# Down projections of combinations 4 to 7 in seven half products, with chunk 10 finished ahead of the loop and chunk 11 in its first pair

## What is computed

```python
Wg = dequant_nvfp4(gate_W_packed, gate_scales)   # [4096, 512]
Wu = dequant_nvfp4(up_W_packed, up_scales)       # [4096, 512]
Wd = dequant_nvfp4(down_W_packed, down_scales)   # [512, 4096]
gate = jnp.einsum('th,nh->tn', xt, Wg)
up = jnp.einsum('th,nh->tn', xt, Wu)
gelu = jnp.tanh(0.7978845608028654 * (gate + 0.044715 * gate ** 3)) * gate * 0.5 + gate * 0.5
inter = gelu * up
out = jnp.einsum('tn,hn->th', inter, Wd)
```

## Time and profile before

| | |
|---|---|
| median of 3 runs | 1121.4 us (1120.69 to 1121.43) |
| profiled execution, its own time | 1121.95 us |
| its span, first to last instruction | 1119.8 us |
| TensorE busy | 1109.5 us, 99% of the span |
| VectorE, GpSimd, ScalarE busy | 851.6, 651.0, 492.9 us |
| granted TensorE clock, mean | 1.000 |
| chain that ended last | 93% TensorE |

### The profile page before, as it was taken

How to read it: one execution, slowest core, us unless ns; L and a number is a source line. 1 busy time by engine, 2 the same in 40 slices (tenths; PEclk the granted TensorE clock), 3 DMA queues, 4 the chain that set the end, 5 groups by cost and what they waited for, 6 DMA issues and landing times.

```text
span 1119.8 us, 22346 instructions
## 1 busy us (share of the span) xinstructions
PE 1109.5 (99%) x8842; PEld 864.5 (77%) x8842; DVE 851.6 (76%) x1491; ACT 492.9 (44%) x1148; POOL 651.0 (58%) x665
## 2 busy tenths in 40 slices
PE   8999999999999999999999999999999999999999
PEld 5666656556457677788888888888888888888886
DVE  7788666457777766688988898889888888886664
ACT  4442344254244344444544455445444544454332
POOL 2376545137684765656775577567756775676330
PEclk9999999999999999999999999999999999999999
DMA  9021111000112222223322232323232323231222
GB/s 307 5 69 47 38 34 42 11 10 1 38 57 76 76 103 103 83 107 115 123 96 105 104 114 95 109 100 114 95 127 88 116 102 126 94 115 76 76 76 76
DMA packets 30232, 96.65 MB, mean 86 GB/s; under 512 B 3440, under 2 KB 3760, under 8 KB 23472
## 3 DMA queue, kind: packets, MB, share of 16 engines
q1 hardware_dynamic: 30128, 95.23, 24.1%
HBM read 63.73 MB, written 31.49 MB: 85 GB/s over the span
## 4 chain that ended last, share of the span: by engine, by line
PE 93%; POOL 2%; DVE 2%; issue 2%; ACT 1%; DMA 0%; SPq 0%; DVEq 0%; POOLq 0%; ACTq 0%
PE ps L627 44%; PE ps L696 19%; PE ps L457 9%; PE ps L588 7%; PE ps L736 7%; PE ps L423 1%; PE ps L549 1%; PE ps L532 1%; PE ps L556 1%; PE ps L543 1%; PE ps L467 1%; PE ps L523 1%; DMA WR<-wqkv 0%; POOL WR L1669 0%; DVE wf L1358 0%
## 5 line engine op out<-in xcount | busy, mean ns | idle before, releaser
L627 PE MATMUL ps<-XT,WR 128*128 128x256 f16 x1344 | 183.3, 273 | 0.0
L627 PE MATMUL ps<-REG,WR 128*128 128x256 f16 x1344 | 183.3, 273 | 0.0
L1020 ACT COPY load<-ps 128x256 f32<-128x256 f32 x168 | 62.4, 371 | 225.6 <-PE ps L627 225.2
L627 PEld LDWEIGHTS ps<-REG,WR 128*128 128x128 f16 x1344 | 130.0, 98 | 21.0
L627 PEld LDWEIGHTS ps<-XT,WR 128*128 128x128 f16 x1344 | 131.5, 98 | 15.4
L1303 DVE SCALAR_TENSOR_TENSOR X<-ps,X 128x512 f32<-128x512 f32 x161 | 108.2, 684 | 16.1 <-PE ps L696 13.8
L1020 ACT COPY bigB<-ps 128x256 f32<-128x256 f32 x168 | 62.5, 372 | 129.4 <-PE ps L627 129.4
L1591 POOL TENSOR_TENSOR ihl_s<-fw,ihl_s 128x512 f16<-128x512 f32 (+1 forms) x46 | 49.5, 1088 | 116.7 <-ACT ihl_s L923 116.7
L1375 DVE TENSOR_TENSOR bigB<-bigB,ps 128x256 f32<-128x256 f32 x168 | 69.7, 415 | 59.8 <-ACT bigB L1020 37.0
L1375 DVE TENSOR_TENSOR load<-load,ps 128x256 f32<-128x256 f32 x168 | 68.8, 414 | 45.3 <-ACT load L1020 31.8
L627 PE MATMUL ps<-REG,bigA 128*128 128x256 f16 x672 | 91.7, 273 | 1.0 <-ACT bigB L1020 1.0
(11 more groups left out here) (231 smaller groups left out, 2515.5 us busy)
## 6 DMA issues: line engine op xcount, KB each, us to landing
kept<-X SPq DMA_DIRECT2D x26, 1024.0 KB, 4.5
X<-kept SPq DMA_DIRECT2D x26, 1024.0 KB, 5.7
load<-codes SPq DMA_DIRECT2D x48, 256.0 KB, 2.7
load<-scales SPq DMA_DIRECT2D x48, 256.0 KB
bigA<-cla SPq DMA_DIRECT2D x14, 256.0 KB, 3.1
X<-x SPq DMA_DIRECT2D x3, 1024.0 KB, 13.0
WR<-wqkv SPq DMA_DIRECT2D x2, 1024.0 KB, 9.8
y<-X SPq DMA_DIRECT2D x2, 1024.0 KB, 4.8
```

Of the source, the lines that this page charges most:

```text
L627: mm = eng.matmul(half_bank(kind, name), w(wp, kt), x(xp, kt), start=(first and n == 0), stop=(n == 5), skip_group_check=True)
L1020: eng.copy(start, half_bank(kind, name)).then_inc(s_snap, 1)
```

## The change

Combinations 4 to 7 join those whose down work is done in seven half products. For this chunks 10 and 11 get the form of the other down chunks: chunk 10 is of the first kind and is finished ahead of the loop (codes between tiles 13 and 14, scalings behind tile 15 on VectorE; cast on ScalarE and low half on GpSimd as the last thing ahead of the loop), and chunk 11 gets the sums and is finished in pair 8, its sums in pair 9. The counts of pairs of chunks, the two float buffers that chunks use in turn, the loads and the release of bank 7 follow.

```diff
-SEVEN = tuple(range(8, 31))
+SEVEN = tuple(range(4, 31))
...
 def plain(k):
 
-    return k < 6 or k in (10, 11, LAST)
+    return k < 6 or k == LAST
...
 def pair_count(k):
 
-    return k % 6 // 2 + 1 + (3 * (k // 6) - 4 if k >= 12 else 0)
+    return 3 * (k // 6 - 1) + k % 6 // 2 + 1
 
 def finished_in(k):
 
-    return k - 2 if k < 12 else 8 * (k // 6) + (-6, -5, -3, -2, -1, 0)[k % 6]
-
-FINISHED = {finished_in(k): k for k in range(10, 48)}
+    return 8 * (k // 6) + (-6, -5, -3, -2, -1, 0)[k % 6]
+
+FINISHED = {finished_in(k): k for k in range(11, 48)}
 
 def second_before(m):
 
     g = m // 8
-    if m % 8 == 1 and m > 9:
+    if m % 8 == 1:
         return 6 * g + 5
...
-            return wfs[pair_count(k) % 2 if k >= 12 else 0]
+            return wfs[1 - pair_count(k) % 2 if k >= 12 else 0]
...
-            return tb[:, :] if k < 6 else PS[7 if k < 10 else 5][:, :].bitcast(I32)
+            return tb[:, :] if k < 6 else PS[7 if k < 11 else 5][:, :].bitcast(I32)
...
-            banks.freed[7] = [(s_dq, 60)]
+            banks.freed[7] = [(s_dq, 66)]
...
@@ ScalarE, dq_mul and dq_first
-                    if g == 1:
-                        ac.wait_ge(s_mm["v"], 16)
-                        ac.wait_ge(s_tlo, 4)
...
+                elif k == 10:
+                    ac.wait_ge(s_tlo, 4)
...
@@ ScalarE, ahead of the loop and in it
             inter_high(15)
+            dequant(10)
             for m in range(8, NI // 2):
...
-                if m < 12 or m % 8 == 7 and m in FINISHED:
+                if m in FINISHED and (m < 12 or m % 8 == 7):
                     dequant(FINISHED[m])
...
@@ VectorE, dq_finish
-                elif k in (12, 14):
+                elif k >= 12:
                     dv.wait_ge(s_kept[1], 16)
-                    dv.wait_ge(s_wlo, WLO[11][1])
-                    dv.wait_ge(s_wsum, 2)
-                elif k > 14:
                     dv.wait_ge(s_wsum, pair_count(k) - 2)
...
@@ VectorE, ahead of the loop and in it
             token_sums(1)
-            for i in range(13, 16):
-                act_tile(i)
+            act_tile(13)
+            dq_bits(10)
+            act_tile(14)
+            act_tile(15)
+            dq_finish(10)
             for m in range(8, NI // 2):
...
                 combine("gate", m, "C12")
                 if m < 12:
-                    dq_bits(FINISHED[m])
+                    if m in FINISHED:
+                        dq_bits(FINISHED[m])
...
                 combine("up", m, "C11")
-                if m < 12:
+                if m < 12 and m in FINISHED:
                     dq_finish(FINISHED[m])
...
@@ GpSimd, ahead of the loop and in it
             token_low(1)
+            dequant(10)
             for m in range(8, NI // 2):
...
-                elif k and k > 11:
+                elif k:
                     if c == 0:
                         dq_difference(k)
                     dq_first_sums(k)
                     dequant(k)
...
@@ SP's queue
             eng.dma_start(kept[2], X1[:, 8:12, :]).then_inc(s_kept[0], 16)
+            load_chunk(11)
...
                 if m < 12:
-                    load_codes(m + 3)
-                    load_scales(m + 3)
+                    if m in FINISHED:
+                        load_chunk(FINISHED[m] + 1)
```

More of the change, by code:

```diff
@@ L987, in dq_sums @@
                     ac.wait_ge(s_kept[(g + 1) % 2], 16)
-                    ac.wait_ge(s_tlo, 16)
+                    if g % 2 == 0:
+                        ac.wait_ge(s_tlo, 16)
                 if k == LAST + 1:
```

## The result

The changed kernel takes 1126.5 us (median of 5 runs, 1124.86 to 1127.81), the kernel before 1121.4 (5 runs, 1120.69 to 1121.85). The ratio is 1.0045 [1.0031, 1.0060]: **slower by 5 us**. I had forecast 1123.1 in a range up to 1125.8, so the result lies above the range. The profiled execution took 1126.26 us, span 1124.5, which is 4.7 more than the span before.

A forecast was written before the change was run, and what follows sets the result against it. TensorE's work plus its few gaps was taken as the bound. +4.2 (gap in pair 8) + 1.1 (pairs 10 to 12) - 3.6 (pairs 13 to 17) = +1.7 us, forecast 1123.1 from 1121.4; range 1120.0 to 1125.8.

The forecast's parts named there:

- The matmuls: Half products in place of plain down products in pairs 13 to 17: 68.12 us for 71.75, minus 3.6.
- Chunk 10 ahead of the loop: Pair 8's first snapshot waits behind chunk 10's scalings and cast, so P6 waits from 328.0 to 332.15: plus 4.2 us.
- rival 1: Loop's start: scalings before tile 15 let ScalarE reach the first snapshot in time; sum -3.9, 1117.5 us; chance 0.10.
- rival 3: Behind pair 8's new gap the clock falls and TensorE works slowly: 1.8 us on top, 1124.9 us; chance 0.12.
- +1.1: Pairs 10 to 12: 48.1 us against 47.06, as waits on GpSimd and VectorE outweigh the matmuls saved.
- 4.5 to 6.5 us of waiting: Pairs 11 and 12: TensorE's waiting while GpSimd, working without rest, makes four low halves per pair; 4.8 taken.
- Rival 2: VectorE and GpSimd stretch each other's token and operand sums: 2.4 us more in pairs 10 to 13, 1125.5; chance 0.23.
- P6 some 4 us behind P2: Sign in pair 8: P6 released late by ScalarE's snapshot, with VectorE's scalings of chunk 10 ending near 331.
- Pair 9 at 14.35: Sign that pair 9 keeps its length of 14.35 us, the extra work of chunk 11 being hidden.
- Pair 10 near 15.3: Sign of VectorE's load in pair 10, its last needed sum about 0.9 us late for TensorE.
- Pairs 11 and 12 together near 33: Sign of GpSimd busy from chunk 12's low half to the low halves of pair 11; length in us.
- A stretch behind the gap at half rate: Sign listed as proving the forecast wrong: TensorE at half rate behind pair 8's gap.

The follow-up runs named there:

- cast_late: Changed kernel with ScalarE's cast of chunk 10 moved behind pair 8's three gate snapshots, not ahead of the first; 1123.44 us, ratio 1.0018 to the kernel before.
- gpsimd_early: Changed kernel with GpSimd's token sums of block 3 moved ahead of chunk 12's low half in pair 10; 1125.74 us, ratio 1.0038 to the kernel before.
- chunks_only: Changed kernel with combinations 4 to 7 back in plain down products, chunks 10 and 11 still finished early (output differs); 1127.16 us.
- wait_40: Kernel before with 40 small ScalarE copies ahead of pair 8's first snapshot, to make a gap; 1127.45 us, ratio 1.0050.
- fill_gap: Changed kernel with 30 unused matmuls between P2 and P6 of pair 8, where TensorE waits for the snapshot; 1124.74 us.
- three_split: Changed kernel with chunk 10's cast late, GpSimd's block 3 sums early, VectorE's token sums in pairs 9 and 12 in two halves; 1120.43 us.
- late_spread: Changed kernel with chunk 10's cast behind pair 8's gate snapshots and VectorE's token sums four at a time in pairs 9 and 12; 1127.00 us.
- all_three: Changed kernel with chunk 10's cast late, GpSimd's block 3 sums early, and VectorE's token sums four at a time in pairs 9 and 12; 1123.92 us.

## Why the prediction was wrong

I forecast 1123.1; measured 1126.5. Step by step, against the profiled execution, whose sum I had put at +1.7 and which came out at +4.7.

**The matmuls.** -3.6 for pairs 13 to 17: measured 71.75 - 68.12 = 3.63. Right.

**Chunk 10 ahead of the loop.** +4.2 with P6 at 332.15; P6 came at 331.58 with the pair's start 0.47 earlier, so the gap is 4.04. The order of the chain, scalings, cast, snapshot, P6, was as worked out. Right, and rival 1 (cover at the loop's start) with it excluded. What I had not seen is that a part of the gap's price doesn't come back with its removal: without the gap (cast_late) pairs 9 to 12 grow by 2.1 us. That doesn't move the forecast, but whoever reads a gap's length as what its removal gives is wrong by 2 us here.

**The clock.** This is the first step that failed: rival 3, to which I gave 0.12, is what happened. I had worked out its price from the transposes as 1.8; the profile shows 1.68. That the price came so near is partly luck: three other profiles with such a gap lost 2.7 to 2.9. Nor is its source shown to be the clock: narrow windows of the trace of before, which I had not asked for, give a granted clock of 1.00 from 2 to 6 us too, where the slow transposes stand. The chance was wrong. I had kept it low because no row of the loop had such a gap, which is evidence for neither side. The Trainium skill's sentence (TensorE: Matmul & The Clock Gate, "Why this matters for your kernels") said what was to come: an idle gap of some microseconds between bursts of matmuls brings the lower level back. The runs agree with it: each of the four profiles with a gap of 3.4 to 3.6 us in pair 8 (after, gpsimd_early, chunks_only, wait_40) has 0.50 behind it, and fill_gap, with matmuls in the same place, 1.00.

**GpSimd and VectorE in pairs 10 to 12.** The second step that failed is the term "+1.1": measured +2.99. Pair 10 was put at 0.9 above 14.41 and has 1.2, with the wait where I had it. For pairs 11 and 12 I had "4.5 to 6.5 us of waiting ... I take 4.8", and 0.5 beside; they take 34.45, which is 6.9 above 27.51. The low half of pair 11's tile was to be ready 24.2 us after the pair's start if GpSimd was slowed as in the rows of before; TensorE's product that needs it starts at 400.08, 24.3 after 375.76. The end that I named as the upper one was met, though in part by luck: GpSimd began its stretch 0.56 us ahead of the pair and not 0.63 behind its start, and then took 1.3 us longer, since the four sums of token_sums(3) took 5.75 us in place of 4.48. I had moved off that end "since VectorE is less in GpSimd's way", a reason without a row. It was not so: VectorE is busy 16.98 of 17.36 us of that pair. Rival 2 (the two in each other's way, +2.4) comes close in size, and a part of its mechanism is there: the three operand sums from 378.40 take 3.98 us, 1.2 more than the 2.8 that I had counted. How much of TensorE's waiting comes from that, and how much from the sheer work, no run separates. Of the places of the waits I had some: 386.75 waits for GpSimd through the gelu, as 379.23 did before, and 400.08 for the low half. The start of pair 12 waits 1.06 us for token_low(2), which I didn't name, and in pair 11 two waits (0.68 and 1.03) are for VectorE's sums, for which I had put nothing.

**The sum.** +4.04 + 1.68 + 0.15 + 2.99 - 3.63 = +5.2, less 0.5 by which pair 8 began earlier: +4.7. Of the 3 us by which the profile misses the forecast's 1.7, the clock is 1.7 and pairs 10 to 12 are 1.9; 0.5 goes the other way. I had treated rivals 2 and 3 as ways that exclude each other, with 1125.5 and 1124.9; both came true at once, and the range had no case for their sum, 1123.1 + 2.4 + 1.8 = 1127.3.

**Signs that I had named.** "P6 some 4 us behind P2": 3.38 us of waiting, right. "Pair 9 at 14.35": 14.50. "Pair 10 near 15.3": 15.60. "Pairs 11 and 12 together near 33": 34.45. "A stretch behind the gap at half rate" was listed as what would prove me wrong, and did.

What stays open: how long and where the clock falls in the other runs of the changed kernel. They differ by 3 us, wider than those of the kernel before. The profiled run has a mean clock of 0.997, and its two stretches at half clock are 6.9 us together. By the same measure, an estimate, the run with 0.995 (1127.81 us) had some 11 us at half clock and the one with 0.998 (1124.86 us) some 4 or 5, but only one execution has a trace.

## What to carry to other kernels

Before work is put ahead of a loop on an engine that takes its instructions in order, follow the first instruction behind it to TensorE: here one cast, 0.5 us long but 2.7 us in waiting for VectorE, opened a gap of 4 us, and the gap opened a stretch at half clock that cost 1.7 to 2.9 more. Matmuls taken out are worth only what the engines that feed TensorE can follow: of 4.8 us, 0.6 arrived, since GpSimd and VectorE are the bound in three of the eight pairs, in two of them already before the change. Mishaps that don't exclude each other add up, so the range needs the case in which two of them come together.

## What the runs showed of the hardware

*The price of a fall differs for like gaps.* Behind 3.38 us without work the clock was at 0.50 until 335.5 in one profile (1.68 us lost), and until 336.2 to 337.2 in two others with 3.4 us (2.7 and 2.80 us lost) and in the one with 3.58 (2.89). In these three the granted clock was already below 1 in the gap itself (0.68 at 330 in wait_40), in the first only behind it.

*For shorter waits the traces go either way.* No fall behind waits of 0.60 and 1.72, nor behind 2.22 (fill_gap), 2.52 (three_split) and one of 2.40 (late_spread); a fall behind another of 2.40 and behind 3.16 (both all_three), and behind another of 2.22, which follows one of 1.82 seven us earlier (late_spread). Two waits of about 1 us, 1.9 apart, were followed by a fall in the changed kernel and not in fill_gap.

*Four token sums in a row on VectorE, each with two SBUF inputs, took 5.8 and 6.3 us beside a working GpSimd*, some 1.5 each, and two took 3.14 and 3.25; in the kernel before two took 1.41 three times and 3.19 once. The Trainium skill (SBUF — State Buffer, "SBUF: two separate sides") has such an instruction and one of GpSimd exclude each other for their whole length. These rows agree with it. Not every pair of sums beside a busy GpSimd is stretched in full, though: this one took 1.98, while GpSimd worked without rest from 383.42 to 388.33.

```profile
384.22 1.98 DVE L1365 TENSOR_TENSOR WR<-WR 128x512 f32<-128x512 f32 x2
```
